# Four 128-token jobs for the last stage of batches 6 and 7, with the product of outer table and masked row on VectorE

## The chip, the cores and the metric

One core of one Trainium2 chip runs the whole program. The metric is the device time of one execution in microseconds, the median of several runs. The kernel before was run three times.

## What is computed

A residual network of four pairs of layers on x of 2048 tokens with 128 features (8 batches of 256 tokens). Each layer adds f(layernorm(x)) to x: spiking attention and an FFN with 4-bit quantised values; four Mamba layers (a scan over time) and a ternary FFN; linear attention and a mixture of eight experts; a convolution layer and, last, the product-key expert FFN that the change touches:

```python
def _L3_ffn_ref(hidden_states, W_up, W_down, W_q, keys, down_embed, up_embed):
    # HEADS = 4, NUM_KEYS = 64, K = 8
    q = einsum('btd,ed->bte', hidden_states, W_q)      # then split: 2 halves x 4 heads
    sim = einsum('pbthn,hkpn->pbthk', q, keys)
    scores_xy, idx_xy = top_k(sim, K)                   # 8 best of 64 keys in each half
    all_scores = sx[..., :, None] + sy[..., None, :]    # 8 x 8 sums
    all_idx    = ix[..., :, None] * nk + iy[..., None, :]
    scores, pk = top_k(all_scores, K)                   # 8 best pairs of each head
    de, ue = down_embed[indices], up_embed[indices]     # 512 experts
    w = silu(einsum('btd,bthkd->bthk', hidden_states, de) * softmax(scores))
    return einsum('bti,di->btd', silu(hidden @ W_up.T), W_down) + einsum('bthk,bthkd->btd', w, ue)
```

## The kernel before, in words

**Lines of work.** The program consists of jobs (a stage on one batch) in lines. Line F ("front") and line S ("scan") take the 32 units of the Mamba layers (8 batches by 4 layers). Lines a and b (`Os`) take everything else: line a the even batches, line b the odd ones, each job after the one before. Each line has its own semaphores, two PSUM banks (`T.banks`) and a piece of SBUF. After the units of batches 6 and 7 are through, these two batches still go through five stages, L1Ffn, L2Attn, L2Ffn (the experts; 16 steps of hidden, L1444 and L1448, and down, L1456), L3Attn and L3Ffn, batch 6 on line a and batch 7 on line b.

**Order of the queues.** Each stage is a generator for each engine; a `yield` ends a piece of work. `ORDER` holds one string for each of the five engines: `a3b2` means three pieces of line a, then two of line b. An engine executes its queue in just this order, so a piece that waits holds up all that is behind it. The strings were written by a planner outside the kernel.

**The last stage, L3Ffn (L1560 to L1782).** It takes 256 tokens. The norm (L353, L356 on VectorE, L362 to L367 on GpSimd, L372 on ScalarE), its transpose (L378) and the queries (L1730, copied at L1682) are for all 256. The rest goes block by block of 128 tokens, i = 0 and 1, in the same buffers. TensorE makes the similarities (L1739, copied at L1688) and the products with down_embed (L1743) in bank `o`; VectorE takes the eight best of 64 (MAX8 L1589), their indices (L1593), the differences (L1596 to L1599), the 64 sums as products of exponentials (L1607), their eight best (L1612) and the mask (L1614); GpSimd takes the masked row (L1649); VectorE its sum and reciprocal (L1617, L1619). Then for each of four heads h: GpSimd forms the 8x64 outer table of exponentials `Em` (L1665, 512 elements a token), VectorE the masked row `md` (L1630: 1 where the table reaches the eighth best, times down_embed's product from PSUM), GpSimd the product `Em = Em * md` (L1670), ScalarE its SiLU (L1707), and TensorE transposes it and adds it up over the heads in bank `a` (L1768), as a matmul with the identity. `Em` has two buffers, `md` one. L1715 with L1636 handle one column (expert 511) that the table can't hold directly. ScalarE copies the sum (L1718, `wT`), TensorE multiplies with up_embed (L1774), VectorE adds to X (L1639). The dense part is L1751, L1694, L1757, L1603. SyncE writes 256 tokens out when both blocks are done.

The transposes elsewhere (L378, L441, L446) use `e.transpose`; only L1768 is written as `e.matmul(..., ident)`.

## Time and profile before

| | |
|---|---|
| median of 3 runs | 1815.65 us (1812.27 to 1816.45) |
| span of the profiled execution | 1807.1 us |
| its own time beside the span | not given; the median lies 8.55 us above the span |
| instructions | 27511 |
| mean granted TensorE clock | 0.897 of full speed |

Busy times are for an engine over the span or a stretch of it. Durations of TensorE records are modelled at their end, so the distance of starts tells more than a single record. A float32 matmul shows as two records, a float32 transpose as one. "Releaser" is what ended an engine's idle time.

### The profile page before, as it was taken

Reading aid. Unit: us, or ns where it says so; the run is one execution under the profiler, and the core shown is the slowest. Engines: PE = TensorE matmul, PEld = TensorE weight load, DVE = VectorE, ACT = ScalarE, POOL = GpSimd, SP = SyncE. Lnnn points to the kernel's source line nnn. Section 1 sums busy time; section 2 is a strip of 40 time slices with the busy share of each in tenths; the row PEclk is TensorE's granted clock in tenths of the full one; section 3 lists DMA queues with packets and bytes.
Section 4 is the critical chain, followed back from the end, with each engine's and each line's share of the span. In section 5 each row is a group of like instructions: output and inputs, shape, how many; then the busy total and the mean of one; then the engine's idle time right before and its main releaser. Section 6 shows DMA issues by size and latency. Waiting matters only on the chain.

```text
span 1807.1 us, 27511 instructions
## 1 busy us (share of the span) xinstructions
PE 1480.0 (82%) x9545; PEld 1061.4 (59%) x9545; DVE 1436.8 (80%) x2200; ACT 1338.4 (74%) x2742; POOL 1210.7 (67%) x999
## 2 busy tenths in 40 slices
PE   5677677667899996676879999689899977899975
PEld 2343333345677775444557777566677755677854
DVE  4679999999988899889998778887998998611154
ACT  4468657757998887786788878798998887744453
POOL 4148659876777688886667667887778978800055
PEclk9678768778999998687999999899999988899987
DMA  5023412523443542221444543242544513122200
GB/s 198 1 71 72 117 39 82 117 71 107 128 135 95 173 117 58 71 71 39 117 119 127 147 121 93 59 137 72 162 106 136 158 47 92 47 83 74 99 1 6
DMA packets 84585, 170.10 MB, mean 94 GB/s; under 512 B 9440, under 2 KB 14944, under 8 KB 84064
## 3 DMA queue, kind: packets, MB, share of 16 engines
q1 hardware_dynamic: 84448, 168.36, 33.4%
q8 instruction: 76, 1.25, 0.3%
q14 instruction: 61, 0.50, 0.1%
HBM read 99.11 MB, written 2.10 MB: 56 GB/s over the span
## 4 chain that ended last, share of the span: by engine, by line
PE 46%; DVE 21%; ACT 17%; POOL 8%; issue 5%; DMA 2%; SPq 0%; DVEq 0%; POOLq 0%; ACTq 0%
DVE m L1052 9%; ACT m L1027 5%; PE ps L1444 5%; PE ps L966 5%; PE ps L1456 5%; DVE dtuB L1044 4%; ACT L345 4%; PE ps L1081 3%; PE ps L1183 3%; PE ps L1315 3%; POOL o L1670 2%; POOL o L1665 2%; PE ps L713 2%; ACT o L670 2%; PE ps L700 2%
## 5 line engine op out<-in xcount | busy, mean ns | idle before, releaser
L1062 POOL TENSOR_TENSOR m<-m 128x1024 f32<-128x1024 f32 x256 | 768.9, 3008 | 84.8 <-DVE m L1052 84.4
L1052 DVE TENSOR_TENSOR_SCAN m<-m,dtuB 128x1024 f32<-128x1024 f32 x256 | 584.9, 2285 | 18.6 <-ACT m L1027 5.6
L1027 ACT ACTIVATE m<-m,Aneg 128x255 f32<-128x255 f32 x1024 | 427.6, 497 | 24.5 <-DMA m<-m 23.2
L1044 DVE TENSOR_TENSOR dtuB<-m 128x1024 f32<-128x1024 f32 x256 | 342.5, 1338 | 13.1 <-DMA m<-m 5.0
L345 ACT ACT_TABLE_LOAD x188 | 241.2, 1283 | 3.3
L362 POOL TENSOR_TENSOR o<-o,mhalf 128x2 f32<-128x2 f32 x64 | 19.7, 308 | 222.1 <-DVE o L356 222.1
L1081 PE MATMUL ps<-m,w_const 128*32 128x256 f32 x2048 | 148.7, 415 | 5.7 <-POOL m L1062 5.7
L1425 ACT ACTIVATE o<-ps,w_mo 128x256 f32<-128x256 f32 x256 | 106.2, 471 | 51.0 <-PE ps L1448 50.9
L1444 PE MATMUL ps<-o 128*128 128x256 f32 x512 | 138.2, 392 | 6.8 <-ACT o L1425 5.2
L966 PE MATMUL ps<-m,wc 128*128 128x256 f32 x512 | 136.2, 425 | 6.2 <-ACT m L383 6.2
L1456 PEld LDWEIGHTS ps<-o 128*128 128x128 f32 x1024 | 128.6, 191 | 16.3 <-issue 4.9
L1456 PE MATMUL ps<-o 128*128 128x128 f32 x1024 | 136.4, 277 | 0.4 <-DMA o<-in_mox 0.3
L1768 PE MATMUL ps<-w_const,o 128*128 128x128 f32 x512 | 90.0, 340 | 55.8 <-DVE o L1636 36.1
L1183 PE MATMUL ps<-o 128*128 128x256 f32 x512 | 121.9, 385 | 10.4 <-issue 5.1
L966 PEld LDWEIGHTS ps<-m,wc 128*128 128x128 f32 x512 | 108.3, 216 | 30.6 <-ACT m L383 10.0
L1768 PEld LDWEIGHTS ps<-w_const,o 128*128 128x128 f32 x512 | 81.7, 245 | 67.6 <-ACT o L1707 45.4
L670 ACT ACTIVATE o<-ps 128x512 f32<-128x512 f32 x112 | 66.3, 593 | 68.2 <-PE ps L713 42.4
L713 PE MATMUL ps<-o 32*128 32x256 bf16 x224 | 55.9, 344 | 74.1 <-ACT o L670 60.9
L1183 PEld LDWEIGHTS ps<-o 128*128 128x128 f32 x512 | 93.2, 190 | 31.5 <-issue 14.8
L1081 PEld LDWEIGHTS ps<-m,w_const 128*32 128x32 f32 x2048 | 70.0, 118 | 70.3 <-issue 26.1
L1444 PEld LDWEIGHTS ps<-o 128*128 128x128 f32 x512 | 88.4, 190 | 26.7 <-ACT o L1425 12.6
L1670 POOL TENSOR_TENSOR o<-o 128x512 f32<-128x512 f32 x64 | 89.2, 1394 | 21.5 <-DVE o L1630 20.4
(246 smaller groups left out, 2783.8 us busy)
## 6 DMA issues: line engine op xcount, KB each, us to landing
m<-m SPq DMA_DIRECT2D x256, 256.0 KB, 4.9
m<-spread SPq DMA_DIRECT2D x64, 512.0 KB, 5.0
o<-in_mox SPq DMA_DIRECT2D x128, 256.0 KB, 3.4
o<-in_l1x SPq DMA_DIRECT2D x88, 256.0 KB, 2.9
w_mb<-in_mb SPq DMA_DIRECT2D x1, 2288.0 KB, 12.1
m<-in_cwr SPq DMA_DIRECT2D x1, 2048.0 KB, 16.0
w_l3f<-in_l3f SPq DMA_DIRECT2D x1, 1536.0 KB, 17.4
X<-in_x SPq DMA_DIRECT2D x4, 256.0 KB, 7.2
```

Source lines behind the costliest of these rows:

```text
L345: e.preload_act_table_set(SETS[kind])
L966: op = e.matmul(b[:, h * CH:h * CH + CH], wc[:, l, j, h * 128:h * 128 + 128], v.xT[:, j:j + CH], start=j == 0, stop=j == 3)
L1027: op = e.activation(dA[at % NA][:, j, 1:CH], R[q][:, h * CH + 1:h * CH + CH], ACT.Exp, scale=Aneg[:, l, 4 * g + j:4 * g + j + 1])
L1044: e.tensor_tensor(dtuB[:, :, :], bc(R[q][:, (2 + h) * CH:(3 + h) * CH].unsqueeze(1), 4, CH), Br[k % 2], ALU.mult).then_inc(S.dve, n.tick(f ...
L1052: e.tensor_tensor_scan(flat(G[at % NG]), flat(dA[at % NA]), flat(dtuB[:, :, :]), 0.0, ALU.mult, ALU.add).then_inc(S.dve, n.tick(f"s{g}"))
L1062: e.tensor_tensor(G[at % NG], G[at % NG], Cr[k % 2], ALU.mult).then_inc(S.pool, n.tick(f"c{g}"))
L1081: op = e.matmul(S.y[32 * q:32 * q + 32, h * CH:h * CH + CH], red, G[(8 * k + g) % NG][:, j, :], start=False, stop=j == 3, skip_group_check ...
L1183: op = e.matmul(b[:, 0:CH], v.ring[(at + j) % RING][:, cut(k)], src[:, k, :], start=k == 0, stop=k == 3)
L1444: e.matmul(b[:, j * CH:j * CH + CH], v.ring[p // 2 * 2 % MRING][:, cut(p % 2 * 2 + j)], v.xT, start=j == 0, stop=False, skip_group_check=True)
L1456: op = e.matmul(a[:, cut(i)], v.hd[p % 2][:, j, cut(i)], v.ring[(p // 2 * 2 + 1) % MRING][:, cut(p % 2 * 2 + j)], start=False, stop=p == 1 ...
L1670: e.tensor_tensor(v.Em[h % 2], v.Em[h % 2], v.md, ALU.mult).then_inc(T.pool, n.tick(f"w{i}{h}"))
L1768: op = e.matmul(a[:, cut(k)], v.Em[h % 2][:, cut(k)], ident, start=h == 0 and k == 0, stop=h == 3, skip_group_check=True)
```

## The change

- Batches 6 and 7 don't run L3Ffn any more. Each gets two jobs of a new stage, L3Half, of 128 tokens each: the first on its own line (a or b), the second on a new line, c for batch 6 and d for batch 7. The new lines use SBUF of the scan and PSUM banks of the scan and the front, which are free by then. So there are four jobs with their own buffers.
- In L3Half VectorE, not GpSimd, makes the product `Em * md`, right behind the mask. L3Half keeps 128 tokens throughout: norm, queries and the dense part too, each with one copy or activation of 512 columns in place of two.
- Batches 0 to 5 keep L3Ffn with GpSimd's product.
- L1768 and its like in L3Half are now transposes (`is_transpose=True`), for all batches.
- Each block of 128 tokens of batches 6 and 7 has its own output transfer.
- All five strings of `ORDER` are new, from their beginning on. Shown are the last lines of those of TensorE and VectorE.

```diff
@@ ORDER @@
     "pe":
...
+        "ba4baba2b2a2bab2abab3a2b3a2b3ababa2ba2ba4babab2aba2baba2b4ab6ab9cb4ab6c3bca3ba2cb6ad5cdb2a2c3ad2cb2abd3",
     "dve":
...
+        "abfa2s3a5safa2fab4ab2a2s3a2b2sbsa2ba2bsbs5b9sa2bs3b2a3fafb6a4b10a6cab2c2b2cba3b2a3dac2acab6c2b3d3cda2dadbc3d3b2d3"
+        "bacd",
+        Ps = [line(f"o{2 + i}") for i in range(2)]
+        for i, T in enumerate(Ps):
+            T.mem = mem[:, i * MO_:(i + 1) * MO_]
+        Ps[0].banks = ps[0:2]
+        Ps[1].banks = [flat(dtuB[:, 2 * i:2 * i + 2, :]) for i in range(2)]
+
+        before, after, ready = [None] * NB, [None] * NB, [None] * NB
...
-                            op = e.matmul(a[:, cut(k)], v.Em[h % 2][:, cut(k)], ident, start=h == 0 and k == 0, stop=h == 3,
+                            op = e.matmul(a[:, cut(k)], v.Em[h % 2][:, cut(k)], ident, is_transpose=True, start=h == 0 and k == 0, stop=h == 3,
...
+        class L3Half(Stage):
...
+                v.Em = [V.get(512) for _ in range(2)]
+                v.md = V.get(512)
...
+            def dve(self, e, n, c, i):
+                v, T = self, self.T
+                a, o = T.banks
+                Xi = X[:, 2 * c + i, :]
+                if n.dve():
+                    e.wait_ge(T.dve, n.dve())
+                else:
+                    e.wait_ge(F.dve, F.done(after[NB - 1][1]))
+                from_, job = ready[c]
+                e.wait_ge(from_.dve, from_.done(job))
+                yield from norm_dve(e, n, T, v, X[:, 2 * c + i:2 * c + i + 1, :])
+                e.wait_ge(T.act, n.act("sm"))
...
+                e.wait_ge(T.dve, n.dve("s83"))
+                e.tensor_tensor(v.msk, v.al, bc(v.s8[:, :, 7:8], 4, 64), ALU.is_ge).then_inc(T.dve, n.tick("mk"))
+                yield
+                e.wait_ge(T.pool, n.pool("e"))
+                e.tensor_reduce(v.sm, v.e64, AX.X, ALU.add).then_inc(T.dve, n.tick("sm"))
+                e.wait_ge(T.dve, n.dve("sm"))
+                e.reciprocal(v.rinv, v.sm).then_inc(T.dve, n.tick("ri"))
+                yield
+                for h in range(4):
+                    if h:
+                        e.wait_ge(T.dve, n.dve(f"W{h - 1}"))
+                    e.wait_ge(T.pool, n.pool(f"E{h}"))
+                    if h == 0:
+                        e.wait_ge(T.pe, n.pe("D"))
+                    e.scalar_tensor_tensor(v.md, v.Em[h % 2], v.s8[:, h, 7:8], o[:, :], ALU.is_ge, ALU.mult).then_inc(
+                        T.dve, n.tick(f"w{h}"))
+                    e.wait_ge(T.dve, n.dve(f"w{h}"))
+                    e.tensor_tensor(v.Em[h % 2], v.Em[h % 2], v.md, ALU.mult).then_inc(T.dve, n.tick(f"W{h}"))
+                    yield
+                    if h == 0:
+                        e.tensor_copy(v.d5, o[:, 511:512]).then_inc(T.dve, n.tick("d5"))
+                e.wait_ge(T.act, n.act("w2"))
+                e.tensor_tensor(v.Em[0][:, 511:512], v.Em[0][:, 511:512], v.w5, ALU.add).then_inc(T.dve, n.tick("a5"))
+                yield
+                e.wait_ge(T.pe, n.pe("ue"))
+                e.tensor_tensor(Xi, a[:, 0:128], Xi, ALU.add).then_inc(T.dve, n.tick("x"))
+                yield
+
...
+            def pool(self, e, n, c, i):
+                v, T = self, self.T
+                norm_pool(e, n, T, v)
+                yield
+                e.wait_ge(T.dve, n.dve("mk"))
+                e.tensor_tensor(v.e64, v.al, v.msk, ALU.mult).then_inc(T.pool, n.tick("e"))
+                yield
+                e.wait_ge(T.act, n.act("ss"))
+                for p in range(2):
+                    if p:
+                        e.wait_ge(T.dve, n.dve("ri"))
+                        e.tensor_tensor(v.e64, v.e64, bc(v.rinv.unsqueeze(2), 4, 64), ALU.mult).then_inc(T.pool, n.tick("r"))
+                        e.wait_ge(T.pool, n.pool("r"))
+                        e.wait_ge(T.dve, n.dve("fl"))
+                        p4 = v.e64.rearrange("p h (a b) -> p (h a) b", b=8)
+                        e.tensor_tensor(p4, p4, bc(flat(v.fl).unsqueeze(2), 32, 8), ALU.mult).then_inc(T.pool, n.tick("p"))
+                        yield
+                    for h in (2 * p, 2 * p + 1):
+                        if p:
+                            e.wait_ge(T.pe, n.pe(f"t{h - 2}"))
+                        Eh = v.Em[h % 2].rearrange("p (a b) -> p a b", a=8)
+                        e.tensor_tensor(Eh, bc(v.s3[:, h, 0:8].unsqueeze(2), 8, 64), bc(v.s3[:, 4 + h, :].unsqueeze(1), 8, 64),
+                                        ALU.mult).then_inc(T.pool, n.tick(f"E{h}"))
+                        yield
...
+            def act(self, e, n, c, i):
...
+                for p in range(2):
+                    for h in (2 * p, 2 * p + 1):
+                        Eh = v.Em[h % 2]
+                        table(e, "silu")
+                        e.wait_ge(T.dve, n.dve(f"W{h}"))
+                        e.activation(Eh, Eh, ACT.Silu, scale=v.rinv[:, h:h + 1]).then_inc(T.act, n.tick(f"w{h}"))
+                        yield
+                    if p == 0:
+                        table(e, "silu")
+                        e.wait_ge(T.pool, n.pool("p"))
+                        e.wait_ge(T.dve, n.dve("d5"))
+                        e.activation(v.pc, v.pc, ACT.Silu, scale=v.d5, accum_out=v.w5).then_inc(T.act, n.tick("pc"))
+                        yield
+                e.wait_ge(T.pe, n.pe("t3"))
+                e.copy(v.wT, a[:, :].rearrange("p (a b) -> p a b", a=4)).then_inc(T.act, n.tick("wT"))
+                yield
...
+            def pe(self, e, n, c, i):
...
+                e.wait_ge(loaded["l3f"], 16)
+                for k in range(4):
+                    op = e.matmul(o[:, cut(k)], w("l3f", "q")[:, cut(k)], v.xT, start=True, stop=True)
+                op.then_inc(T.pe, n.tick("q"))
+                yield
+                e.wait_ge(T.act, n.act("q"))
+                for k in range(4):
+                    op = e.matmul(a[:, cut(k)], v.qT[:, k, :], w("l3f", "keys")[:, k, :], start=True, stop=True)
+                op.then_inc(T.pe, n.tick("sm"))
+                yield
+                e.matmul(o[:, :], v.xT, w("l3f", "de"), start=True, stop=True).then_inc(T.pe, n.tick("D"))
+                yield
...
+                for h in range(4):
+                    e.wait_ge(T.act, n.act(f"w{h}"))
+                    if h == 0:
+                        e.wait_ge(T.dve, n.dve("d"))
+                    if h == 2:
+                        e.wait_ge(T.dve, n.dve("a5"))
+                    for k in range(4):
+                        op = e.matmul(a[:, cut(k)], v.Em[h % 2][:, cut(k)], ident, is_transpose=True, start=h == 0 and k == 0, stop=h == 3,
+                                      skip_group_check=True)
+                    op.then_inc(T.pe, n.tick(f"t{h}"))
+                    yield
+                e.wait_ge(T.act, n.act("wT"))
+                for k in range(4):
+                    op = e.matmul(a[:, 0:128], v.wT[:, k, :], w("l3f", "ue")[:, k, :], start=k == 0, stop=k == 3)
+                op.then_inc(T.pe, n.tick("ue"))
+                yield
...
-                todo += [(T, s, c) for s in (PRE if word[0] == "a" else POST)]
+                todo += [(T, s, c) for s in (PRE if word[0] == "a" else POST if c < NB - 2 else POST[:-1])]
...
+        for c in (NB - 2, NB - 1):
+            T = next(T for T, s, d in todo if d == c and s is L3Attn)
+            ready[c] = (T, len(T.jobs) - 1)
+            T.add(L3Half(T), c, 0)
+            P = Ps[c % 2]
+            P.add(L3Half(P), c, 1)
         Line.listed = True
-        lines = {"u": U, "s": S, "f": F, "a": Os[0], "b": Os[1]}
+        lines = {"u": U, "s": S, "f": F, "a": Os[0], "b": Os[1], "c": Ps[0], "d": Ps[1]}
```

The parts left out of L3Half are those of L3Ffn, for 128 tokens and with no index i: similarities are in bank `a`, down_embed's product in bank `o`.

## Rows read from the trace of the kernel before

**Rows 1.** The page, busy time, share of the span and instructions of each engine:

```profile
PE 1480.0 (82%) x9545; PEld 1061.4 (59%) x9545; DVE 1436.8 (80%) x2200; ACT 1338.4 (74%) x2742; POOL 1210.7 (67%) x999
```

**Rows 2.** Table by stretches: stretch, us, busy (instructions) by engine, clock, DMA share, GB/s:

```profile
700.00:800.00 100.00, 72.16 (x455) 49.69 (x453) 87.21 (x161) 76.42 (x143) 83.80 (x67) 0.78 0.25 65
1100.00:1300.00 200.00, 169.28 (x1101) 129.32 (x1101) 172.58 (x294) 172.66 (x328) 162.30 (x134) 0.96 0.35 94
1400.00:1600.00 200.00, 164.48 (x1027) 126.44 (x1028) 158.70 (x276) 152.17 (x295) 153.39 (x127) 0.89 0.30 83
1600.00:1700.00 100.00, 98.90 (x670) 81.25 (x669) 11.53 (x48) 44.18 (x102) 4.30 (x16) 1.00 0.28 93
1724.80:1730.60 5.80, 5.12 (x18) 3.00 (x17) 3.82 (x9) 2.33 (x4) 2.03 (x2) 0.71 0.02 4
1734.00:1804.00 70.00, 44.40 (x238) 36.82 (x236) 33.70 (x124) 33.83 (x54) 45.71 (x48) 0.80 0.00 0
```

**Rows 3.** The page, chain that ended last, shares of the span by engine:

```profile
PE 46%; DVE 21%; ACT 17%; POOL 8%; issue 5%; DMA 2%; SPq 0%; DVEq 0%; POOLq 0%; ACTq 0%
```

**Rows 4.** Timelines of TensorE, ScalarE and VectorE, last 90 us: start us, us, what:

```profile
1717.90 2.25 PE L1456 MATMUL ps<-o 128*128 128x128 f32 x16
...
1720.84 1.99 PE L1730 MATMUL ps<-o,w_l3f 128*128 128x256 f32 x8 [0.47 <-ACT o L383]
...
1724.61 1.16 PE L1739 MATMUL ps<-w_l3f,o 128*128 128x128 f32 x8 [0.62 <-ACT o L1682]
...
1723.51 1.05 ACT L1682 COPY o<-ps 128x512 f32<-128x512 f32 x2
...
1725.81 0.59 ACT L1688 COPY o<-ps 128x512 f32<-128x512 f32 x1 [0.96 <-PE ps L1739]
...
1801.90 0.59 ACT L1718 COPY o<-ps 128x512 f32<-128x512 f32 x1 [2.16 <-PE ps L1768]
...
1730.60 1.08 DVE L1589 MAX8 o<-o 128x8 f32<-128x64 f32 x8
...
1733.19 0.42 DVE L1519 TENSOR_TENSOR o<-o,w_l3a 128x256 f32<-128x256 f32 x1
...
1734.10 0.49 DVE L353 BATCH_NORM_STATS2 o<-X 128x6 f32<-128x128 f32 x2
...
1803.73 0.29 DVE L1639 TENSOR_TENSOR X<-ps,X 128x128 f32<-128x128 f32 x1 [5.93 <-PE ps L1774]
```

**Rows 5.** Groups by line, 1734 to 1807: xcount, busy us, mean ns, idle before, releasers:

```profile
L1670 POOL TENSOR_TENSOR o<-o 128x512 f32<-128x512 f32 x16 | 20.2, 1265 | 6.0 <-DVE o L1630 6.0
L1665 POOL TENSOR_TENSOR o<-o 128x512 f32<-128x512 f32 x16 | 17.0, 1081 | 4.7 <-PE ps L1768 4.7
L1630 DVE SCALAR_TENSOR_TENSOR o<-o,ps 128x512 f32<-128x512 f32 x16 | 11.9, 746 | 21.8 <-POOL o L1670 12.0 <-POOL o L1665 9.8
L1707 ACT ACTIVATE o<-o 128x512 f32<-128x512 f32 x16 | 11.4, 721 | 18.0 <-POOL o L1670 18.0
...
L1607 DVE TENSOR_TENSOR o<-o 128x256 f32<-128x256 f32 x4 | 2.5, 633 | 0.9 <-ACT o L1698 0.9
...
L1614 DVE TENSOR_TENSOR o<-o 128x256 f32<-128x256 f32 x4 | 2.5, 618 | 0.1
...
L1599 DVE TENSOR_TENSOR o<-o 128x512 f32<-128x512 f32 x3 | 2.0, 682 | 0.0
```

**Rows 6.** One line's instructions over the span: duration ns min/median/max:

```profile
L1607 DVE TENSOR_TENSOR o<-o x16: 408/417/1266, 677.1 to 1784.0; 128x256 f32<-128x256 f32 x16
...
L1044 DVE TENSOR_TENSOR dtuB<-m x256: 1207/1232/3252, 110.4 to 1566.9; 128x1024 f32<-128x1024 f32 x128
```

**Rows 7.** Timeline of GpSimd, the two tables beside which L1607 ran longest:

```profile
1763.43 2.66 POOL L1665 TENSOR_TENSOR o<-o 128x512 f32<-128x512 f32 x2 [2.93 <-PE ps L1768]
```

**Rows 8.** Timeline of TensorE: transposes of L441, and L1768 as matmuls:

```profile
703.29 1.95 PE L1768 MATMUL ps<-w_const,o 128*128 128x128 f32 x16
...
1665.04 0.60 PE L441 MATMUL ps<-w_const,o 128*128 128x128 f32 x4
```

174 lines of the change are left out of this document (127 added, 47 removed).

## The prediction

> **What bounds the kernel now.** I read the busy shares first, then the table by stretches, the chain of waits, and the timelines of the last 90 us. No engine is full over the span: TensorE 82%, VectorE 80%, GpSimd 67% [rows 1]. The stretches show why. While units of the scan run (700 to 800, 1100 to 1300) VectorE is busy 86 us in every 100 and TensorE 72 to 85; from 1600 to 1700 TensorE is at 98.9, the others nearly idle: batches 6 and 7 run alone and are bound by matmuls; in the last 70 us nobody is full: GpSimd 45.7, TensorE 44.4, VectorE 33.7 us [rows 2]. The chain of waits gives TensorE 46% and VectorE 21% of the whole span [rows 3].
>
> The last stage runs thus. Batch 7's expert layer leaves TensorE at about 1720.2; its L3Ffn starts at 1734.10. The last result goes into X at 1803.73 and ends at 1804.0 [rows 4]; the span ends at 1807.1, so 3.1 us are the output's transfer. For these 70 us two lines each work through two blocks of 128 tokens **one after the other**. In each head the outer table (L1665, 1.04 us) and the product (L1670, 1.27 us) are GpSimd's, and between them VectorE's mask (L1630, 0.75 us). VectorE stood idle 21.8 us before L1630, all for GpSimd [rows 5]. GpSimd's 45.7 us in 70 is the sum of four blocks, and the two lines don't hide each other's latencies.
>
> **The change, part by part.**
>
> *Products moved.* Sixteen L1670 leave GpSimd: 16 x 1.265 = 20.2 us [rows 5]. What remains there is 45.7 - 20.2 = 25.5 us: 16 tables of 1.08, the small products, a norm. GpSimd no longer binds.
>
> *What VectorE gains.* No row shows this product on VectorE. The nearest is L1599, two SBUF inputs of 128x512 float32: 0.68 us; L1044 at twice the size, 1.232 us, gives 0.62 as the lower end [rows 6]. The upper end is 0.68 plus a whole GpSimd table, 1.72. I take 0.68, as the form is the same. VectorE's 33.7 us between 1734 and 1804 [rows 2] hold the work of all four blocks and batch 7's norm, but for batch 6's first maxima, indices and subtractions (L1589 to L1599), which ran from 1730.60 to 1733.19 [rows 4]: 2.6 us. Taken off are 1.9 us of port waits (next part), to it come 16 x 0.68 = 10.9: 45.3 us, or 11.3 for a job. (In a job each mask now waits for the product before it, as there is one md; with four jobs another's work can stand between, in part.) L3Attn's instructions for batch 7 share the queue: 3.8 us between 1724.8 and 1730.6 [rows 2], and 0.9 from 1733.19 to 1734.10 [rows 4]: together **50.0 us**.
>
> *The shared way to SBUF.* L1607 takes 0.417 us as a rule and 1.266 at worst, L1044 1.232 and 3.252 [rows 6]. The worst case lies at 1763.92, under the two tables that GpSimd ran from 1763.43 to 1766.09 [rows 7]; L1630, with one operand in PSUM, kept its 0.75 throughout [rows 5]. In the last 73 us the four L1607 average 633 and the four L1614 618, the three L1599 682 [rows 5]: against 0.42 and 0.68 that is 1.7 us too much over 11 instructions; with small ones 1.9, some 0.17 each. The change has 28 such instructions (L1599, L1607, L1614, four products, in four jobs): 4.8 us. The Trainium skill, "SBUF — State Buffer", section "Who interferes with whom", says that a VectorE instruction with two SBUF inputs and a GpSimd instruction that reads SBUF exclude each other, for the whole instruction; by that, with GpSimd busy 25 of 55 us and half a table left on average, the term would be 28 x 0.45 x 0.52 = 6.5 us, an estimate that needs the page. The trace agrees with the rule.
>
> *Four jobs instead of two times two.* The new orders put c (batch 6, second block) first on VectorE, then a, and b and d from L3Attn's end on. On TensorE, c's queries follow the last expert step of batch 7, so nothing starts sooner than 1720.2. The old path had the first similarities copied at 1725.81 + 0.59 [rows 4]; half the queries' columns (1.16 for 1.99) and one copy of 0.59 for two (1.05) bring this to 1725.1. From there VectorE always has one of four jobs. Walking its order through, I find about 3.3 us idle, mainly where a's last column waits for ScalarE's third SiLU. The cover is thin: VectorE is then the binding engine, and each us added to it is a us of time.
>
> *The end.* After the last product: SiLU 0.77, transposes 0.9 at the lower clock, and from the copy of wT to the result 2.15 as now (1801.90 to 1804.02) [rows 4]: 3.8 us (0.77 is L1707's 0.72 [rows 5] and the hand-over; 0.9 is an estimate, one group at half the clock); then 3.1 for the transfer. Four output transfers of 64 KB replace two of 128 on SyncE; three of them lie before the last and cost nothing.
>
> *L3Attn b delayed.* c's maxima and indices (1.8 us) stand before parts of batch 7's L3Attn on VectorE. That is in the sum, since VectorE is counted as one queue; what waits behind L3Attn there is only b and d.
>
> *Orders of the body.* The strings let batch 6 lead batch 7 by six expert steps more. A batch alone leaves short gaps on TensorE between its steps, so batch 7 ends later: I allow 1.0 us, between 0 and 2.25, the time of the last two groups of L1456 [rows 4].
>
> *Sum of the last stage:* 1725.1 + 50.0 + 4.8 + 3.3 + 3.8 + 3.1 + 1.0 = **1791.1**, that is 16.0 us under 1807.1. Without idle, port waits and the later start: 1782.0 (25.1 gained). If each of the 16 products waited for a whole table: 1791.1 + 16 x (1.04 - 0.17) = 1805.0 (2.1 gained).
>
> *Transposes.* L1768 becomes a transpose for all batches. As matmuls 16 records need 1.95 us, 0.112 each, two to a 128x128 block; L441's transposes take one record, four in 0.60 us [rows 8]. Each group of four falls from 0.90 to 0.45 us; 64 groups: 28.7 us of TensorE, 21.5 of them in batches 0 to 5. There TensorE has slack, so most is hidden; the upper end is 46% (its share of the chain), 9.9 us, the lower end 0. I take 4, nearer the lower end, since in the stretches with L3Ffn (700 to 800, 1100 to 1300, 1400 to 1600) it is at 72 to 85%.
>
> *All queues are reordered* from the first unit on, SyncE's and GpSimd's too. The trace doesn't price that. "Issue" holds 5% of the chain, 90 us [rows 3]; I bound the effect by a tenth of that, 9 us to either side, and take 0.
>
> Total: 16.0 + 4 = 20.0 us. The profiled execution's own time isn't given beside its span; the median of the three runs is 1815.65, 8.55 above the span, and I take this as what lies around it: 1815.65 - 20.0 = **1796**, 1.1% less.
>
> **Rivals.** *(1) The port eats it.* The products collide with tables of other jobs, which now run any time. For: both engines are busy for most of 55 us, and VectorE binds. Against: 0.17 us is all that 11 instructions show. Time: 2.1 + 4 gained, 1809.6; it holds the band 1804 to 1812. Chance 0.14.
>
> *(2) More is won.* Little idle and few collisions, and the body uses its 21.5 us: 25.1 + 9.9 gained, 1781. For: VectorE's idle time before L1630 falls away also as a rule. Against: a fixed order never fits exactly. Chance of under 1788: 0.18.
>
> *(3) Slower: the clock of TensorE falls in the body.* The stretches 1100 to 1300 and 1400 to 1600 have 334 us of TensorE work at a granted clock of about 0.92, and 700 to 800 shows that such a stretch can stand at 0.78 [rows 2]. With fewer columns there, 0.78 throughout would make the work 18% longer, 60 us, 46% of it on the chain: 28 us, so 1796 + 28 = 1824. It decides from 20 us on, a clock of about 0.81. For: TensorE idles more when each group is halved. Against: each time it is only 0.45 us less, among long runs of matmuls. The Trainium skill, "TensorE: Matmul & The Clock Gate", Part 4, says that transposes don't count as activity the way matmuls do; by it the 64 groups would be gaps altogether, and the fall likelier. No row here shows that: the old transposes stand too thin. Chance 0.08.
>
> *(4) No difference.* The new order of the body loses more than the 9 us that I allow, some 16 to 20, against the last stage's gain; or the four jobs are held by one wait in a fixed queue, such as d's norm behind c's tables on GpSimd. 1812 to 1819.3. Chance 0.08.
>
> **How the numbers follow.** The forecast, 1788 to 1804, has 0.52. The range, 1779 to 1811, reaches from rival 2's end to rival 1's, with 1 to 2 us for the spread of the runs (1812.27 to 1816.45); left out are the slower and unchanged cases, 0.16, and a sliver at either end. A measurement of this kernel tells about 0.2% (3.6 us) from no change. Faster: 0.52 + 0.18 + 0.14 = 0.84; same 0.08; slower 0.08.
>
> **What would show it.** In the new profile: the last result some 43 to 50 us after the start of batch 7's L3Ffn, not 70; VectorE above 80% busy there; GpSimd near 25 us in all; products at 0.68 with some at 1.2 to 1.7; transposes with one record a block, 0.45 us a group; no change of more than a few us up to batch 7's entry. It would be wrong if that entry moved from 1734 by over 5 us, if products averaged over 1.2 us, or if VectorE stood idle over 10 us in the last stage.

## The result: slower by 8.6%

The changed kernel takes 1972.62 us (median of 4 runs, 1969.22 to 1974.73), the kernel before 1814.6 us beside it (4 runs, 1812.27 to 1816.45). The ratio is 1.0862, 95% interval 1.0835 to 1.0889. Forecast were 1796 us and a range of 1779 to 1811. The last stage did nearly what was forecast; the body, to which the prediction gave 0 us, lost some 180 in its scan part.

The page of the changed kernel, first its busy shares, then the chain that ended last:

```profile
PE 1515.0 (77%) x9321; PEld 1072.1 (54%) x9321; DVE 1467.6 (74%) x2218; ACT 1330.3 (68%) x2736; POOL 1176.2 (60%) x991
...
PE 46%; ACT 21%; DVE 14%; DMA 6%; POOL 6%; issue 5%; SPq 3%; DVEq 0%; ACTq 0%; POOLq 0%
```

No engine has much more work than in [rows 1]: TensorE +35, VectorE +31, ScalarE -8, GpSimd -35 us. The span of the traced execution went from 1807.1 to 1970.0 us, so every share fell. (Executions of one kernel differ by several us, and the traced one of the kernel before is a quick one: in every other run of this record the time lies 1.7 to 3.7 us above the span, so it took some 1809 to 1811 us, by an estimate from these, where the median is 1814.6.) Time that belongs to no engine's work is waiting. In the chain VectorE lost 7 points against [rows 3]; DMA came up from 2 to 6% and SyncE's queue from 0 to 3%.

The table by stretches, columns as in [rows 2]:

```profile
1100.00:1300.00 200.00, 176.80 (x1195) 136.49 (x1193) 152.24 (x235) 154.18 (x328) 127.90 (x111) 0.97 0.39 105
1400.00:1600.00 200.00, 173.40 (x1150) 130.60 (x1149) 160.34 (x161) 154.21 (x332) 128.29 (x80) 0.92 0.41 116
1600.00:1700.00 100.00, 71.83 (x462) 53.38 (x461) 82.38 (x170) 72.59 (x141) 76.26 (x71) 0.88 0.26 78
```

VectorE has 152 us of work in 1100 to 1300 where it had 173. At 1600 to 1700, where before only matmuls of batches 6 and 7 were left, scan units still run. The last scan starts at 1752.1 us (1573.74 before). The lag grows at every unit, and about evenly: unit 0 starts 6.8 us late, unit 8 41.7, unit 16 90.1, unit 24 133.9, the last scan 178.4.

The page's costliest groups and the list of waits (us in total, times, longest) name the place of it. First groups of the changed kernel:

```profile
L1070 POOL TENSOR_TENSOR m<-m 128x1024 f32<-128x1024 f32 x256 | 761.5, 2982 | 171.1 <-DVE m L1060 113.4
L1060 DVE TENSOR_TENSOR_SCAN m<-m,dtuB 128x1024 f32<-128x1024 f32 x256 | 584.9, 2285 | 47.0 <-ACT m L1035 22.3
...
L1052 DVE TENSOR_TENSOR dtuB<-m 128x1024 f32<-128x1024 f32 x256 | 355.8, 1390 | 44.6 <-DMA m<-m 23.0
```

The same lines before:

```profile
L1062 POOL TENSOR_TENSOR m<-m 128x1024 f32<-128x1024 f32 x256 | 768.9, 3008 | 84.8 <-DVE m L1052 84.4
L1052 DVE TENSOR_TENSOR_SCAN m<-m,dtuB 128x1024 f32<-128x1024 f32 x256 | 584.9, 2285 | 18.6 <-ACT m L1027 5.6
L1044 DVE TENSOR_TENSOR dtuB<-m 128x1024 f32<-128x1024 f32 x256 | 342.5, 1338 | 13.1 <-DMA m<-m 5.0
```

And the changed kernel's waits on the two transfers of the scan:

```profile
POOL m L1070 <- DMA m<-spread: 57.4, 10, 14.7
ACT m L1035 <- DMA m<-m: 37.9, 13, 6.5
DVE dtuB L1052 <- DMA m<-m: 23.0, 11, 5.5
```

The instructions of the scan last as long as before (a scan 2285 ns in both). What stands before them has grown: 84.8 to 171.1 us, 18.6 to 47.0, 13.1 to 44.6. Two kinds of transfer are late: `m<-spread`, which gives B and C of a unit to all partitions, and `m<-m`, the eight "rows" of a unit. Before, the list of waits has 23.2 us of ScalarE and 5.0 of VectorE for rows, and for a spread a single wait of VectorE's, 1.4 us. The transfers themselves last hardly longer (from issue to landing 5.0 us in the median for a row transfer, 4.9 before; 6.1 for a spread, 5.0 before), so most of the lateness is that SyncE issues them late.

**The last stage.** The timeline of VectorE in the changed kernel, from batch 7's last expert addition on:

```profile
1903.57 0.42 DVE L1411 TENSOR_TENSOR X<-ps,X 128x256 f32<-128x256 f32 x1 [16.05 <-PE ps L1464]
...
1907.48 1.11 DVE L1824 MAX8 m<-m 128x8 f32<-128x64 f32 x8 [2.75 <-ACT m L1912]
...
1943.66 1.56 DVE L1864 TENSOR_TENSOR o<-o 128x512 f32<-128x512 f32 x1
...
1961.79 0.69 DVE L1864 TENSOR_TENSOR m<-m 128x512 f32<-128x512 f32 x1
...
1967.73 0.29 DVE L1872 TENSOR_TENSOR X<-dtuB,X 128x128 f32<-128x128 f32 x1 [2.44 <-PE dtuB L1983]
```

From that addition to the end of the last result it is 64.5 us; before it was 83.8 (1720.19 to 1804.02). That is 19.4 us less; the forecast had 16.0. Between the first maximum and the last product VectorE is nearly full, GpSimd is not. The table by stretches:

```profile
1907.48:1962.48 55.00, 34.22 (x188) 28.65 (x189) 50.24 (x166) 32.70 (x56) 34.42 (x42) 0.75 0.00 1
```

So the loss up to the end of batch 7's L2Ffn is 1903.57 - 1720.19 = 183.4 us, and 183.4 - 19.4 = 164 is the difference of the two results' ends.

### The profile page after: what moved, and what is told of

It is laid out like the page before. It is cut to its first block, busy times and chain, and to the rows that moved or that the text cites. A ratio compares the mean times of both kernels' runs of the same rounds, so it can differ in the third digit from the quotient of the medians.

```text
span 1970.0 us, 27068 instructions
## 1 busy us (share of the span) xinstructions
PE 1515.0 (77%) x9321; PEld 1072.1 (54%) x9321; DVE 1467.6 (74%) x2218; ACT 1330.3 (68%) x2736; POOL 1176.2 (60%) x991
## 3 DMA queue, kind: packets, MB, share of 16 engines
q8 instruction: 75, 1.23, 0.3%
## 4 chain that ended last, share of the span: by engine, by line
PE 46%; ACT 21%; DVE 14%; DMA 6%; POOL 6%; issue 5%; SPq 3%; DVEq 0%; ACTq 0%; POOLq 0%
ACT m L1035 5%; PE ps L974 5%; DVE m L1060 5%; PE ps L1452 4%; PE ps L1089 4%; ACT L351 4%; PE ps L1464 3%; PE ps L1323 3%; PE ps L1191 3%; DVE dtuB L1052 3%; POOL m L1070 2%; DMA m<-m 2%; ACT o L678 2%; PE ps L721 2%; PE ps L708 2%
## 5 line engine op out<-in xcount | busy, mean ns | idle before, releaser
L1070 POOL TENSOR_TENSOR m<-m 128x1024 f32<-128x1024 f32 x256 | 761.5, 2982 | 171.1 <-DVE m L1060 113.4
L1060 DVE TENSOR_TENSOR_SCAN m<-m,dtuB 128x1024 f32<-128x1024 f32 x256 | 584.9, 2285 | 47.0 <-ACT m L1035 22.3
L1052 DVE TENSOR_TENSOR dtuB<-m 128x1024 f32<-128x1024 f32 x256 | 355.8, 1390 | 44.6 <-DMA m<-m 23.0
L370 POOL TENSOR_TENSOR o<-o,mhalf 128x2 f32<-128x2 f32 (+1 forms) x64 | 22.4, 349 | 260.1 <-DVE o L363 260.0
L1452 PE MATMUL ps<-o 128*128 128x256 f32 x512 | 142.9, 403 | 20.9 <-DMA o<-in_mox 10.4
L974 PE MATMUL ps<-m,wc 128*128 128x256 f32 x512 | 145.0, 445 | 12.5 <-ACT m L391 12.5
L1464 PEld LDWEIGHTS ps<-o 128*128 128x128 f32 x1024 | 131.4, 194 | 21.9 <-DMA o<-in_mox 5.2
L1191 PE MATMUL ps<-o 128*128 128x256 f32 x512 | 127.2, 400 | 20.8 <-DMA o<-in_l1x 10.3
L974 PEld LDWEIGHTS ps<-m,wc 128*128 128x128 f32 x512 | 113.5, 227 | 39.8 <-ACT m L391 17.2
L1191 PEld LDWEIGHTS ps<-o 128*128 128x128 f32 x512 | 99.4, 200 | 41.9 <-issue 13.5
L678 ACT ACTIVATE o<-ps 128x512 f32<-128x512 f32 x112 | 66.3, 594 | 81.4 <-PE ps L721 44.7
L1452 PEld LDWEIGHTS ps<-o 128*128 128x128 f32 x512 | 91.8, 196 | 42.2 <-ACT o L1433 17.5
L721 PEld LDWEIGHTS ps<-o 32*128 32x128 bf16 x224 | 13.4, 99 | 138.8 <-ACT o L678 96.9
L903 POOL TENSOR_TENSOR m<-m 128x512 f32<-128x512 f32 x32 | 45.5, 1421 | 69.7 <-DVE m L868 69.7
L1277 ACT ACTIVATE o<-ps 128x512 f32<-128x512 f32 x64 | 37.9, 593 | 72.7 <-PE ps L1323 72.5
```

The lines of the kernel that those rows point to most:

```text
L721: op = e.matmul(score[h % len(score)][:, kt * CH:kt * CH + CH], v.km[j][32 * g:32 * g + 32, cut(kt)], v.qk[32 * g:32 * g + 32, 0, :], star ...
L974: op = e.matmul(b[:, h * CH:h * CH + CH], wc[:, l, j, h * 128:h * 128 + 128], v.xT[:, j:j + CH], start=j == 0, stop=j == 3)
L1052: e.tensor_tensor(dtuB[:, :, :], bc(R[q][:, (2 + h) * CH:(3 + h) * CH].unsqueeze(1), 4, CH), Br[k % 2], ALU.mult).then_inc(S.dve, n.tick(f ...
L1060: e.tensor_tensor_scan(flat(G[at % NG]), flat(dA[at % NA]), flat(dtuB[:, :, :]), 0.0, ALU.mult, ALU.add).then_inc(S.dve, n.tick(f"s{g}"))
L1070: e.tensor_tensor(G[at % NG], G[at % NG], Cr[k % 2], ALU.mult).then_inc(S.pool, n.tick(f"c{g}"))
L1191: op = e.matmul(b[:, 0:CH], v.ring[(at + j) % RING][:, cut(k)], src[:, k, :], start=k == 0, stop=k == 3)
```

## The experiments

All strings are written out below as SyncE meets them: x, B and C are a unit's transfer to the scratch rows and its two spreads, 0 to 7 its eight rows, a and b pieces of the two lines. "Body" is everything up to the last stages of batches 6 and 7.

**1. Is it the body's order? (e1, e3)** e1 is the changed kernel with all five strings in their old order up to batch 7's expert step 10, and the new tail. e3 is the opposite: the stages of before, with the new order up to the same place.

```diff
 e1, SyncE's first units
-ux0B1234567CxB01234567CxB01234567CxB01234567CxBC01234567x...
+uxBC01234567xBC01234567xBC01234567xB0C1234567xBC01234567x...
```

> The changed kernel with the old order of all five queues up to batch 7's expert step 10 and the new order from there; stages and transposes as changed. Theory A (the new order of the body costs some 5.6 us in each of the 32 scan units, the last stage gains): 1795 to 1802 us, last scan at about 1570 us of the span. Rival B (the transposes lower the clock or otherwise slow the body): stays at 1940 to 1973. Rival C (only the order of the DMA queue): like A here; e4 tells them apart.

> The kernel before (two-block L3Ffn, GpSimd's product, matmul with the identity) with the changed kernel's order up to batch 7's expert step 10, old order after it. Theory A: 1814.6 + 178 less 0 to 5 = 1985 to 1995 us, each scan unit 5.6 us longer. Rival B: 1810 to 1825. Rival C: as A.

e1: 1807.1 us (1800.9 to 1812.62), ratio 0.9939 (0.9911 to 0.9966), 5 us above theory A's upper end. e3: 1987.51 us, one run, as theory A had it. With the new last stage and the old order the kernel is faster than before; with the old last stage and the new order it loses some 170 us. The order of the body is the whole loss, and e3, which has no transposes, rules these out as its cause. In e1 the last stage from batch 7's addition to the end takes 62.6 us, 21.2 less than before, but the place where the two orders meet (the "seam") costs: from the last scan to that addition 157.8 us against 146.5. TensorE is idle for 12.0 us of it, before for 3.2.

**2. The transposes alone (e2).** The kernel before, with one edit:

```diff
-    op = e.matmul(a[:, cut(k)], v.Em[h % 2][:, cut(k)], ident, start=...
+    op = e.matmul(a[:, cut(k)], v.Em[h % 2][:, cut(k)], ident, is_transpose=True, start=...
```

> The kernel before with L1768 as a transpose and nothing else. Theory A: 1805 to 1816 us (my 4 us of gain, ends 0 and 9.9). Rival B: over 1900 us, with a lower granted clock around the L3Ffn stages.

1821.89 us (10 runs), ratio 1.0022 (1.0008 to 1.0036): 4 us slower, where 4 us of gain were forecast; neither theory of the expectation held. Groups by line, 1100 to 1300, first of e2, then of before:

```profile
L1768 PE MATMUL ps<-w_const,o 128*128 128x128 f32 x64 | 11.3, 317 | 8.9 <-DVE o L1636 6.9 <-ACT o L1707 2.0
```

```profile
L1768 PE MATMUL ps<-w_const,o 128*128 128x128 f32 x128 | 18.8, 301 | 6.0 <-DVE o L1636 5.2 <-ACT o L1707 0.7
```

The instructions are halved and their busy time falls from 18.8 to 11.3 us in this stretch, so the saving itself is real. Over the whole span the line falls from 90.0 to 53.1 us, more than the 28.7 us of the prediction. The granted clock tells where a part of it may have gone; the same stretches of e2:

```profile
1100.00:1300.00 200.00, 165.66 (x1021) 123.41 (x1019) 167.95 (x295) 166.30 (x322) 156.61 (x135) 0.90 0.31 85
1400.00:1600.00 200.00, 160.24 (x981) 118.33 (x982) 171.87 (x287) 157.02 (x305) 160.55 (x129) 0.87 0.31 84
```

Against 0.96 and 0.89 in [rows 2]. One trace of each is weak support: e7 below, which has the matmuls, shows 0.92 and 0.91 in the same stretches. All executions say more. The mean clock over the span was 0.869 to 0.883 in e2's ten, and 0.884 to 0.896 in the fourteen of the kernel before beside them. By the Trainium skill, "TensorE: Matmul & The Clock Gate", Part 4, transposes don't count as activity as matmuls do; e2 agrees. It would agree as well if the clock fell only because TensorE has less work: no run here tells the two apart.

**3. Which queue? (e4, e5)** e4 is the changed kernel with only SyncE's string old. e5 is e1 with only SyncE's string new.

> The changed kernel with only SyncE's queue in the old order; the four compute engines keep the new one. Rival C (the order of the transfers alone makes each unit late: B and C spreads and the replicated rows): most of the 178 us comes back, 1800 to 1850 us. Theory A in its other form (the compute queues' order does it): 1950 to 1975.

> The kernel of e1 (changed kernel, old order of the body on every queue) with SyncE's queue alone put into the new order. e1 measured 1807.1 us. Theory SP: the new string of SyncE issues the spread transfers of B and C behind rows of their own unit and so makes each scan unit wait; by e4 (1923.96 us against 1972.6 of the changed kernel) that is worth 48.7 us, so this run gives 1845 to 1860 us. Rival, compute order: SyncE's string costs only where the other queues are in the new order too (it was laid out for them), then 1805 to 1825 us; or it fits the old order worse than its own, then over 1870 us.

e4: 1923.96 us (one run, between its two theories). e5: 1923.61 us, ratio 1.0606 (1.0568 to 1.0645). With e1 and the changed kernel that makes a table of four:

| us | SyncE old | SyncE new |
|---|---|---|
| other four queues old | 1807.1 (e1) | 1923.6 (e5) |
| other four queues new | 1924.0 (e4) | 1972.6 (changed) |

SyncE's string costs 116.5 us by itself, far over the 38 to 53 that the theory had for e5; the rival that it fits the old order worse than its own came true. The other four's order alone costs 116.9, by the single run of e4; the waits for transfers there are nearly those of before (ScalarE 28.2 us and VectorE 4.3 for rows, none for a spread), so that part has another cause. Together they cost 165.5, not 233. A likely reading, not shown, is that a unit that already waits for one thing doesn't wait twice. e5's waits name the same two transfers:

```profile
POOL m L1071 <- DMA m<-spread: 52.6, 11, 8.0
ACT m L1036 <- DMA m<-m: 45.6, 17, 6.3
DVE dtuB L1053 <- DMA m<-spread: 30.3, 6, 8.9
```

**4. What in SyncE's string? (e6, e9, e10, e11)** e6 mends the changed kernel: spreads B and C go ahead of their unit's rows. e9 to e11 spoil e7 (below; 1803.47 us, all queues old) in steps. In e9 only C is late: by the final strings it is moved in 19 units and stands behind a row of its own unit in 27 of 32, for 12 in e7 (the expectation's 15, 25 and 10 were miscounted). In e10 fronts and scans are among themselves as in the new order, in e11 the feed-forward pieces a and b take their new places.

```diff
 first unit of SyncE's string, e9
-uxBC01234567
+uxB01234567C
 pieces 95 to 127 (units 8 and 9), e10: fronts and scans new
-2aa34567aaaaxBaa0bbaC1ab234567bbb
+2aa34567aaaa01aaxbba23ab4B5C67bbb
 the same pieces, e11: a and b moved
-2aa34567aaaaxBaa0bbaC1ab234567bbb
+123456a7aaaaaxBaa0C12345bb67babbx
```

> The changed kernel with the new order on all queues; in SyncE's string alone the pieces that issue the spread transfers of B and C stand ahead of the rows of their own unit (C behind the unit's first row in 7 of 32 units instead of 25). Theory SP by its place of the spreads: 1920 to 1940 us, most of the 48.7 us that SyncE's old string gave back. Rival, SyncE's string costs by the stores and loads that its head waits for, whatever the place of the spreads: 1960 to 1985 us. Rival, the rows are what the units lack and now come later still: over 1985 us.

> The kernel of e7 (1803.5 us, all queues in the old order of the body) with one thing changed in SyncE's string: in 15 of the 32 units the piece that issues the spread of C stands as many rows further back as in the new order (it stands behind the unit's first row in 25 units instead of 10). Theory place of C: GpSimd's first product of each such unit waits for the spread, and so do the sum in TensorE and the next front; by e5 (SyncE's whole new string on the old order: +116 us over e1) this gives 1850 to 1910 us. Rival, it is the rows and the copies of the feed-forward stages whose places cost: 1803 to 1825 us.

> The kernel of e7 with SyncE's string changed: pieces of the fronts and of the scans stand among themselves as in the new order (x, B, C and the 8 rows of each unit), the pieces of the feed-forward stages stand at their old places, counted in front and scan pieces. Theory: the whole 116 us of e5 come from how spreads and rows are interleaved, 1890 to 1930 us, and the next kernel (e11) is then near 1810 us. Rival: half and half, 1840 to 1880 us in both. Rival: this one near 1810 us, then e11 has it all.

> The kernel of e7 with SyncE's string changed the other way: front and scan pieces among themselves as before, the pieces of the two feed-forward stages (copies and weight loads of the two expert rings) at their places of the new order, counted in front and scan pieces. If the interleaving of spreads and rows is the cause: 1800 to 1820 us. If it is where the feed-forward pieces stand (a copy whose TensorE result is late blocks the rows behind it): 1870 to 1930 us, and e10 is near 1810 us.

| | us | over its base | ratio to before, 95% |
|---|---|---|---|
| e6 (base: changed kernel) | 1945.78 | -26.8 | 1.0729 (1.0693 to 1.0764) |
| e9 (base e7) | 1831.77 | +28.3 | 1.0086 (1.0064 to 1.0108) |
| e10 (base e7) | 1881.07 | +77.6 | 1.0358 (1.0335 to 1.0380) |
| e11 (base e7) | 1889.61 | +86.1 | 1.0405 (1.0380 to 1.0429) |

The bases were measured in another round (the kernel before beside e7 took 1815.2 us, beside e9 to e11 1816.3), so a difference carries a us or two. The place of C is a cause, but a quarter of SyncE's 116.5 us. e6 and e9 came out between their theories and those of their rivals. e10 and e11 are 1 and 10 us above the top of "half and half" (1880), and like e4 and e5 they don't add: 77.6 and 86.1 make 116.5 together. The waits of e9, then of e11, beside e7's, show that each edit makes the wait that it should:

```profile
POOL m L1071 <- DMA m<-spread: 56.6, 11, 8.5
ACT m L1036 <- DMA m<-m: 27.0, 11, 5.8
```

```profile
ACT m L1036 <- DMA m<-m: 45.8, 19, 11.0
DVE dtuB L1053 <- DMA m<-m: 17.2, 7, 8.2
```

```profile
ACT m L1036 <- DMA m<-m: 23.5, 8, 5.6
```

With C's spread issued behind its rows GpSimd waits 56.6 us for it, and the kernel takes 28.3 us more. A row issued behind a feed-forward copy, which itself waits for TensorE, costs ScalarE 22.3 us more than in e7. e10 has late spreads of B too (behind a row of their unit in 13 units, in e7 in 6): GpSimd waits 43.1 us and VectorE 34.6 for spreads in it.

**5. A version that beats both, and its parts (e7, e8, e12).** e7: the old order of the body, the pieces of batch 6's two jobs placed in it by the count of batch 7's pieces, four jobs, product on VectorE, no transposes. e8: e7 with the product on GpSimd again. e12: e7 with the transposes.

```diff
 e8, VectorE, in L3Half
-    e.wait_ge(T.dve, n.dve(f"w{h}"))
-    e.tensor_tensor(v.Em[h % 2], v.Em[h % 2], v.md, ALU.mult).then_inc(T.dve, n.tick(f"W{h}"))
 e8, GpSimd, in L3Half (h is 0 and 1 ahead of the third table, 2 and 3 behind the fourth)
+    e.wait_ge(T.dve, n.dve(f"w{h}"))
+    e.tensor_tensor(v.Em[h % 2], v.Em[h % 2], v.md, ALU.mult).then_inc(T.pool, n.tick(f"W{h}"))
```

> Old order of the body on all queues, with the half pieces of batch 6's last stage put in place by the count of batch 7's pieces, four jobs in the last stage of the last two batches, product on VectorE, and the matrix products with the identity as they were (no transposes). e1 lost 7 to 10 us at its seam (from the last scan to batch 7's add of its feed-forward stage 157.8 us against 146.5 before) and won 21.2 us behind it. Theory: the last stage wins about 19 us, the seam costs 0 to 5 us, and leaving out the transposes gives some 4 us: 1792 to 1802 us, ratio 0.986 to 0.992. Rival: the seam is as dear as in e1 or the last stage lacks its four jobs of batch 6 at the right time: 1803 to 1810 us.

> The kernel of e7 with the product of outer table and masked row back on GpSimd in all four jobs: the four jobs alone. In the span of the kernel before, GpSimd's product took 2.66 us, VectorE's own about 0.7 us in e1. Theory: the four jobs bring the most and GpSimd's product (8 x 1.3 us for 128 columns, beside VectorE) costs 0 to 4 us over e7. Rival: four jobs with GpSimd's product wait for it at every job, and the end is 5 to 12 us later than in e7. Second rival: VectorE is the bound, and taking 8 products of 0.7 us off it makes this kernel 3 to 6 us faster than e7.

> The kernel of e7 with the change's transposes put back (both places where 16 or 4 products with the identity become transposes). By e2 the transposes in the body cost 4.0 us (ratio 1.0022 alone): 1805 to 1811 us, with a lower granted clock in the body. Rival: e2's 4 us was drift between runs and the shorter transposes win as forecast: 1797 to 1802 us.

e7: 1803.47 us (1797.45 to 1809.13), ratio 0.9936 (0.9914 to 0.9959). e8: 1813.68 us, ratio 1.0002 (0.9985 to 1.0019). e12: 1805.86 us (1800.96 to 1810.54), ratio 0.9942 (0.9925 to 0.9959).

So e7 is 0.6% faster than before. That is at the lower edge of its rival (1803 to 1810), not in the 1792 to 1802 expected. The move of the product is worth 10.2 us, as e8's first rival had it (5 to 12), and the four jobs by themselves bring nothing. (The 2.66 us for GpSimd's product in e8's expectation were misread: that is two tables in [rows 7]; one product takes 1.27 us in [rows 5].) The stretch from batch 7's L3Attn to the last result, of e7 and then of e8 (table by stretches):

```profile
1752.30:1805.20 52.90, 35.63 (x230) 31.50 (x230) 43.30 (x125) 30.08 (x52) 31.25 (x36) 0.84 0.02 4
```

```profile
1739.80:1804.00 64.20, 42.04 (x230) 36.89 (x230) 33.65 (x109) 30.77 (x52) 47.18 (x52) 0.76 0.01 4
```

It took 70.8 us before (1733.2 to 1804.02). Four jobs with GpSimd's product: 64.2, 6.6 less; with VectorE's: 53.0, another 11.2 less. In e8 GpSimd has 47 us of work in 64 and VectorE's mask waits for it; groups by line of e8 in that stretch:

```profile
L1862 DVE SCALAR_TENSOR_TENSOR o<-o,ps 128x512 f32<-128x512 f32 x8 | 5.9, 742 | 10.8 <-POOL o L1903 7.3 <-POOL o L1898 2.0 <-POOL o L1886 1.4
L1862 DVE SCALAR_TENSOR_TENSOR m<-m,dtuB 128x512 f32<-128x512 f32 x4 | 3.0, 747 | 6.8 <-POOL m L1898 4.0 <-POOL m L1886 1.4 <-POOL m L1903 1.4
L1862 DVE SCALAR_TENSOR_TENSOR m<-m,ps 128x512 f32<-128x512 f32 x4 | 2.9, 736 | 3.7 <-POOL m L1903 3.7
```

That is the same wait as in [rows 5]: 21.3 us before the 16 masks, 21.8 before. In front of this stretch e7 and e8 take 5.7 and 6.8 us more than before (last scan to batch 7's L3Attn: 165.2 and 166.3 for 159.5). This keeps e7 from the full 17.8 us, but only about half of it is the seam: TensorE is busy 155.4 us there in e7 and 156.4 in e8 for 152.6 before (1016 records for 974), mostly work of batch 6's jobs that before came later (the second block's similarities, 8 records, and the dense part's last product, 16 records and 2.05 us), and idle 9.8 and 9.9 us for 6.8. From the last scan to the last result, which holds both, it is 230.3 us before, 230.5 in e8, 218.2 in e7 and 215.9 in the changed kernel. Such stretches can be compared between traces, ends can't: the last scan of e7's trace starts 13.6 us later than e8's though the orders are the same, for the one is the slowest of e7's six executions (1809.13 us, clock 0.884) and the other the quickest of e8's twelve (1807.75 us, 0.896).

e12 is as its theory had it (1805 to 1811), but it and e7 can't be told apart: 2.4 us, intervals that overlap. In their traces the clock is nearly alike (0.95 from 900 to 1300 in both; 0.88 for 0.90 from 500 to 900), while TensorE's busy time falls by 6.8 us in the first and by 5.3 in the second of these stretches. So the transposes save busy time and none of it is seen at the end. The trace of e7 is of its execution with the lowest clock, though. Over all executions the clock is lower with transposes here too: 0.878 to 0.886 in e12's six (median 0.884; the kernel before beside them 0.890), 0.884 to 0.897 in e7's six (median 0.895; before beside them 0.893).

**6. What in the other queues? (e13 to e18)** A whole compute queue in the new order beside the others in the old wasn't run. But the two orders differ in short stretches with equal counts on both sides, and these can be swapped one by one. e13 swaps 102 of 103 of VectorE's, e14 95 of 178 of ScalarE's, e15 48 of 154 of TensorE's, e16 all of these and 41 of 42 of GpSimd's. e17 is a control: neighbouring pieces of VectorE swapped at random. e18 is every third of its swaps. Pieces 400 to 450 of VectorE's queue (s is a scan piece, f a front piece):

```diff
-sbbsssbsssssssssaassafasassaasfssffsssssssssssfaaa  (e7)
+bfssssbsssssssssaassafaasssaasfssffsssssssssssfaaa  (e13)
+ffsbbssssssssassasssaafassaasfsfssssfssssssssfsaaa  (e17)
+sbbsbsssssssssssaassafaasssaasffssfsssssssssssfaaa  (e18)
```

> The kernel of e7 (1803.5 us) with VectorE's queue alone in the new order of the body, in 102 of the 103 stretches in which the two orders differ (355 of 1138 pieces moved, 0.5 places in the mean). By e4 the order of the four compute queues is worth 117 us beside SyncE's. If VectorE's head of queue is where the units lose (in e4 its front pieces waited 30.0 us for TensorE and 24.3 for ScalarE): 1840 to 1880 us. If the new order hurts only as a whole, or by TensorE's and ScalarE's queues: 1800 to 1815 us.

> The kernel of e7 with ScalarE's queue alone in the new order, in 95 of 178 stretches that differ (320 of 1250 pieces moved, 0.4 places in the mean). If a place or so on one queue is enough to cost: 1820 to 1850 us. If not: 1800 to 1812 us.

> The kernel of e7 with TensorE's queue alone in the new order, in 48 of 154 stretches that differ (196 of 1244 pieces moved, 0.3 places in the mean). If a place or so on one queue is enough to cost: 1815 to 1845 us. If not: 1800 to 1812 us.

> The kernel of e7 with the three above and GpSimd's queue (41 of 42 stretches) together, SyncE's old. If each queue's shift costs by itself and they add, as halves of SyncE's did (28 of C, 78, 86, and 116 for all): about the sum of the three's costs over e7, up to e4's 117 us. If what costs is a mismatch between the queues, then less than the largest of the three.

> Control for e13. The kernel of e7 with VectorE's queue alone shaken at random: neighbours of different stages swapped by a random draw that knows nothing of the new order, 328 of 1138 pieces moved, 0.37 places in the mean (e13: 355, 0.52, +75 us). Theory: any place or so off costs, for each queue of before is fitted to the others: 1845 to 1880 us. Rival: the new order of VectorE is bad in a way of its own: under 1825 us.

> Every third of the random swaps of e17: 105 pieces moved, 0.12 places in the mean. If each swap costs alike and they add: a third of e17's cost. If a few swaps carry it all: anything from 1803 us to e17's time.

| | us | over e7 | ratio to before, 95% |
|---|---|---|---|
| e13 VectorE | 1878.26 | +74.8 | 1.0352 (1.0319 to 1.0384) |
| e14 ScalarE | 1918.59 | +115.1 | 1.0574 (1.0486 to 1.0662) |
| e15 TensorE | 1880.80 | +77.3 | 1.0366 (1.0323 to 1.0408) |
| e16 all four | 1945.25 | +141.8 | 1.0721 (1.0670 to 1.0772) |
| e17 VectorE, 328 pieces at random | 1966.86 | +163.4 | 1.0835 (1.0732 to 1.0938) |
| e18 VectorE, 105 pieces at random | 1858.19 | +54.7 | 1.0236 (1.0139 to 1.0333) |

No single queue carries the loss. Any one that departs from the old order by 0.3 to 0.5 places in the mean costs 75 to 115 us, and all four 142. These are not shares of the 116.9 us that the whole new order of the four costs in e4: e16 moves fewer pieces (on ScalarE 320 for 714, on TensorE 196 for 720) and costs more. So a part of these prices is likely that the changed queues no longer fit each other or SyncE's. The control answers the open question: one random draw of swaps on one queue cost about as much as the whole new order does on five, and a third of them costs a third (54.7 / 163.4 = 0.33). The expectations held for e13 and e18 and were too low for e14, e15 and e17; e16 met neither of its theories: it lies between "the sum" (267) and "less than the largest" (115), and above e4's 117. For VectorE the new order is thus not bad in some way of its own (its 355 moved pieces cost less than half of the random 328); what costs, as I read it, is that the queues leave an order in which each piece meets its inputs just in time. No such control was run for the other queues. The page of e17 shows where it is lost:

```profile
L1071 POOL TENSOR_TENSOR m<-m 128x1024 f32<-128x1024 f32 x256 | 754.4, 2953 | 185.7 <-DVE m L1061 185.4
L1061 DVE TENSOR_TENSOR_SCAN m<-m,dtuB 128x1024 f32<-128x1024 f32 x256 | 584.8, 2284 | 17.8 <-ACT m L1036 7.1
```

GpSimd waits 185.4 us for VectorE's scan (85.7 in e7), while the scan itself never waits long. VectorE comes to the scan late, because it stood before some other piece. One of its waits in e17, then in e7:

```profile
DVE m L849 <- PE ps L1090: 36.4, 11, 7.2
```

```profile
DVE m L849 <- PE ps L1090: 12.2, 11, 3.4
```

L849 is the front's first piece, which needs the sum of an earlier unit. Ahead of its time it blocks VectorE for 36.4 us in place of 12.2, and the scans behind it in the queue. It is the largest of many: VectorE's idle time over the span rises from 357.2 to 476.6 us, 24.2 of it here, then 11.8 before L1129 (for ScalarE) and 8.5 before L361 (for ScalarE). How the 142 us of e16 divide over pieces wasn't resolved. The latencies of a unit tell that it isn't one place. Means over 30 units, from starts and ends in the traces (e7's, not in the table, lie within 0.3 us of the kernel before's):

| us | before | e5 (SyncE new) | e14 (ScalarE new) | changed |
|---|---|---|---|---|
| end of a unit's scans to the front's first piece (L840 before) | 7.4 | 9.1 | 9.0 | 9.1 |
| `hs` of unit k to TensorE's convolution of unit k+2 | 9.5 | 10.7 | 10.1 | 11.5 |
| end of `dt` (VectorE) to the first scan of its unit | 11.2 | 13.4 | 12.6 | 13.8 |
| start of the first to end of the last scan of a unit | 38.9 | 41.6 | 41.9 | 42.7 |
| end of the last scan of k to the first of k+1 | 5.7 | 7.3 | 6.5 | 7.4 |

The last two rows add up to a unit's time, 44.6 before and 50.2 in the changed kernel, 5.5 us more before rounding. Over the 31 units behind the first that is 172 us, and with the 6.8 us that unit 0 is late it is the lag at the last scan, 178.4.

## Why the prediction was wrong, step by step

- **"All queues are reordered ... I bound the effect by a tenth of that, 9 us to either side, and take 0."** This is the step that failed. Its size was 165 us: 1972.6 of the changed kernel against 1807.1 of e1, the same kernel with the old body. The 5% of "issue" is time in which an engine waits for nothing that is seen; it says nothing of a piece that stands behind another in a queue. Two numbers would have given a wide upper end: VectorE is busy 86 us in 100 while units run, so little waits long in the order of before, and there are 32 units of 44.6 us each; a delay of 1 us a unit is 32 us. The prediction named rival 4 (order of the body) with "some 16 to 20" us and no case above it. It also didn't follow what the change does to SyncE's string piece by piece. That the spreads of C stand behind a row in 25 of 32 units, in place of 12, can be read from the strings; e9, with 27 against 12, costs 28 us.
- **Rival 3 (slower, by the clock)** had the right sign and not the mechanism. The mean granted clock fell from 0.897 to 0.852, but in the stretches that it named the changed kernel had 0.97 and 0.92 (before, the same stretches held work that comes over 100 us later, by the lag). e1, with the same transposes and the old body, has 0.884 and none of the loss; e3, without the transposes, has all of it. The clock followed; it didn't cause.
- **"The strings let batch 6 lead batch 7 ... 1.0 us."** From batch 6's expert addition to batch 7's it was 20.2 us before (1700.0 to 1720.19) and 32.9 in the changed kernel (1870.63 to 1903.57); from the last scan to batch 7's addition 151.5 us for 146.5. So 5.0 us and not 1.0, and not by "short gaps on TensorE": it is busy 148.1 us for 143.3, at a granted clock of 0.91 for 0.96, and idle 3.4 for 3.2.
- **The last stage** was right: 19.4 us gained (16.0 forecast, with that 1.0 taken off) in the changed kernel, 21.2 in e1; counted from the last scan, with the 5.0 us above, the changed kernel gains 14.4. By its terms: VectorE's work and waits (50.0 + 4.8 + 3.3 = 58.1) measured 55.0 from the first maximum to the last product, 50.2 of them busy; idle was 4.8. That the sum came so near is in part luck, for terms missed by up to 3 us to both sides. GpSimd no longer bound: 34.4 us in 55. That is 8.9 more than the 25.5 forecast. Its 16 tables took 1.23 us each and not 1.08 (2.5 us), the small products 2.0 us more; the rest is the norms and L3Attn's instructions, which ran ahead of 1734 before.
- **"I take 0.68"** for VectorE's product, plus 0.17 for the port: 0.85 forecast, 0.89 measured over 16. The upper case, 1.72, came near once (1.56). Beyond 0.68 and 0.42 the products and L1599, L1607 and L1614 took some 3.5 us together, for the 4.8 of the term.
- **"The end ... 3.8 us"**: 5.5 us from the end of the last product (1962.48) to that of the last result (1968.02), 3.9 in e1. The step that it leaves out is ScalarE's queue: the last two SiLUs stood behind another job's copy, which waited 3.07 us for TensorE and ran at 1962.76, so that the last SiLU began at 1964.35. VectorE idled 2.00 us for it (0.35 in e1), then 2.44 for the last matmuls (2.44 in e1). The lower clock that it counted with wasn't there: 0.98 from 1962.48 to 1968.02.
- **"Transposes ... I take 4"**: the sign was wrong. e2 is 4.0 us slower (0.08% to 0.36%), e12 shows no difference. The saving of TensorE's time was larger than forecast (36.9 us for 28.7) and none of it arrived; how much of that is TensorE's slack and how much the lower clock isn't settled. The lower end, "0", was the better choice, and the forecast's "46%, its share of the chain" isn't a price of shorter work in the stretches where other engines bind.
- **"8.55 above the span, and I take this as what lies around it"**: the time lies only 1.7 to 3.7 us above the span in all the other runs; the rest was that the traced execution was a quick one. The forecast is a difference from the median, so nothing hangs on it.
- **"It would be wrong if that entry moved from 1734 by over 5 us"**: batch 7's L3Ffn would have begun some 183 us late. The test was right and was the first thing that the new trace showed.
- The range held no case in which the order costs more than 20 us, and 0.84 for faster was given on the last stage alone.

Not settled: what single pieces of the compute queues cost, whether random swaps on another queue than VectorE's cost as much, and whether an order for the changed kernel exists that saves the 3 us or so of idle TensorE at the seam as well. Shown is that SyncE's string by itself costs 116 us, that part of it is the place of C (28 us), and that departures of VectorE's, ScalarE's or TensorE's queue from the old order cost 75 us or more each.

## What to carry to other kernels

A kernel whose queues are written out in one order by hand or by a planner has its schedule as its main asset: price a change of order by units times microseconds per unit, not by the idle time of before, and measure the same edit under the old order first. When new work is needed at the end, keep the body's strings as they are and splice only the tail (e7: 0.6% faster, where the wholly new order was 8.6% slower). In a DMA queue, read for each transfer what stands ahead of it and what that waits for.
